# Storing result blocks from ScalarE's DMA queue instead of SyncE's, in a relational GNN layer with layer normalisation

## Chip, cores and metric

The kernel runs on one core of a Trainium2 chip. The metric is the device time of one execution in microseconds. The engines are called PE (TensorE), DVE (VectorE), ACT (ScalarE), POOL (GpSimd) and SP (SyncE).

## What is computed

There are 50,000 nodes with 256 features, 12,500 edges in eight relations, sorted by destination. Each node gets its own features, the product with a loop weight, and the sum of the messages of its incoming edges; the row is then normalised.

```
hx = jnp.einsum('ni,rio->rno', x, weight)
msg = hx[edge_type, src]
agg = jax.ops.segment_sum(msg, dst, num_segments=num_nodes)
node_repr = agg * 0.5 ** 0.5 + h_bias + (x @ loop_weight) * 0.5 ** 0.5
out = layernorm(x + node_repr)
```

## The kernel before

Work goes in pairs of tiles of 128 rows. There are three kinds. A main pair (m, 196 of them) takes 256 consecutive rows of x through the loop weight (with the identity added for the residual), the bias and the normalisation. A message pair (g, 53) gathers the sources of 256 edges of one relation each tile, multiplies by the relation's weight and scatters the messages into a table in DRAM. A fix pair (f, 50) redoes the rows that receive messages: it gathers x rows, multiplies, adds the sum of the messages by a matmul with a matrix of equal keys, normalises, and scatters the rows over the output that the main pairs stored before.

The order of the pairs is written out by hand as phases, and every engine walks the same list (`walk` with its own `step`): 66 m; then "gmgmgmm" repeated and "gmm" five times; six m; then f and m in turn ("fm"), and at the end four m and four f. While the first 66 main pairs run, POOL sorts the edges by relation with 98 indirect DMAs (line 647). The m pairs run from rows in blocks of four tiles: block b is the pairs 2b and 2b+1, loaded into `x_in` and finished in `y_out`, both rings of `BLOCK_RING` = 4 blocks. There are 97 full blocks of 512 rows and a last one of 336.

What each engine does for a pair: SP loads blocks of x (line 494), messages (532) and keys (524). POOL gathers (624), scatters messages (715) and fixed rows (664). PE transposes (1170), two pairs ahead of its own multiplication (1193), and adds the messages (1215). ACT copies the transposes out of PSUM (1053), moves messages (1084), carries one row from a fix tile to the next (1068), takes the deviation (1095) and normalises in place (1104), which counts up `normed`. DVE makes the low part of the split (892), adds the bias while moving the product out of PSUM (971 for m, 976 for f), and makes statistics (986, 939) and the factors (918, 928).

SP stores the blocks. In its step for the odd pair of block b it waits until PE has turned that pair, issues the load of block b+4, then waits until block b-2 (`LATE` = 2) is normalised, and issues its store (line 570). After the walk it stores the last two; the last block goes in two parts (567, 568). In a fix step SP waits for the pair's product before it loads the messages of the fix pair four further on, so its steps follow PE's. A store counts up `stored` of its slot. DVE waits for it before it adds into the slot again, four blocks later; POOL waits for it before it scatters fixed rows over rows that the main pairs wrote, and SP at the end. The fix pairs before the last three wait only for blocks long before theirs; the last three wait for all blocks.

Each engine's instructions run in the order in which its step issues them. PE, DVE and ACT hold four products in PSUM (`Y_RING`) between them.

Of the kernel before, what the change touches and what calls it, by code (L numbers as in the profile page):

```python
# [33 lines left out]
P = 128  # L34
# [6 lines left out]
BLOCK_RING = 4  # L41
LATE = 2
# [127 lines left out]
def gnn_layernorm_kernel(nc, x, src, dst, rel, weight, bias, loop_weight, out):  # L170
    N, D = x.shape
# [15 lines left out]
    BROWS = 4 * P  # L187
    BLOCKS = N // BROWS
# [69 lines left out]
    with ExitStack() as ctx:  # L258
# [164 lines left out]
        def block_rows(table, b):  # L423

            return table[bass.ds(b * BROWS, BROWS), :].rearrange("(p t) d -> p t d", t=4)
# [54 lines left out]
        def _(sp):  # L480
# [53 lines left out]
            def step(p):  # L534
                if p.kind == "f":
                    slot = p.fixed("f") % 4
                    following = p.count("f") + 4
                    if p.looped or following < FPAIRS:
                        sp.wait_ge(product, p.count("mgf") + 1)
                        load_messages(following * 2, slot)  # L540
                    if slot == 3:
                        unit = p.turns("f", 4)
                        uslot = (p.fixed("f") // 4) % 2
                        if p.looped or unit + 2 < UNITS:
                            sp.wait_ge(same_built, (unit + 1) * UNIT)
                            load_keys(unit + 2, uslot)
                after_p = p.ahead(5)
                if not p.looped and after_p is not None and after_p.kind == "f" and after_p.count("f") == 0:

                    for i in range(2):  # L550
                        sp.wait_ge(scattered[i], 32 * ((MPAIRS + 1 - i) // 2))
                    for f in range(min(4, FPAIRS)):
                        load_messages(2 * f, f)
                if p.kind != "m" or p.fixed("m") % 2 == 0:
                    return
                b, slot = p.turns("m", 2), (p.fixed("m") // 2) % BLOCK_RING
                if p.looped or b + 4 <= BLOCKS:
                    sp.wait_ge(turned, p.count("mgf") + 1)
                    load_block(b + 4, slot)
                if p.looped or b >= LATE:  # L560
                    store_block(b - LATE, (slot - LATE) % BLOCK_RING, nth(p, "m", -2 * LATE))

            def store_block(b, slot, ends):

                sp.wait_ge(normed, ends.count("mf") + 1)
                if isinstance(b, int) and b == BLOCKS:
                    sp.dma_start(out[b * BROWS:b * BROWS + 2 * P, :].rearrange("(p t) d -> p t d", t=2), y_out[:, slot, 0:2, :]).then_inc(stored[slot], 16)
                    sp.dma_start(out[N - REST:N, :], y_out[0:REST, slot, 2, :]).then_inc(rest_stored, 16)
                else:
                    sp.dma_start(block_rows(out, b), y_out[:, slot, :, :]).then_inc(stored[slot], 16)  # L570

            walk(sp, phases, step)
            end = Pair(phases, len(phases) - 1, 0, phases[-1].size - 1)
            for b in range(BLOCKS + 1 - LATE, BLOCKS + 1):
                store_block(b, b % BLOCK_RING, nth(end, "m", 2 * (b - BLOCKS) - 1))
            sp.wait_ge(rest_stored, 16)
            for i in range(BLOCK_RING):
                sp.wait_ge(stored[i], 16 * ((BLOCKS + BLOCK_RING - i) // BLOCK_RING))
# [464 lines left out]
        @block.scalar  # L1043
        def _(act):
            def copy_xt(p):

                if p is None:
                    return
                n, slot = p.count("mgf"), p.fixed("mgf") % Y_RING
                act.wait_ge(turned, n + 1)  # L1050
                wait(act, product, n - Y_RING + 1)
                to = xt_full if p.plain else xt_high
                nc.scalar.activation(to[:, slot, :], xt_ps[slot % XT_RING][:, :], ACT.Copy).then_inc(copied, 1)  # L1053

            def carry(p, t):

                if p is None or p.kind != "f":
                    return
                if not has_carry(p, t):
                    return  # L1060
                nxt = p if t == 0 else nth(p, "f", 1)
                slot = nxt.fixed("f") % 4
                act.wait_ge(message_loaded[slot], 32 * (nxt.turns("f", 4) + 1))
                if t == 0:
                    act.wait_ge(tile_sum, p.count("f") + 1)
                else:
                    act.wait_ge(product, p.count("mgf") + 1)
                nc.scalar.activation(message_in[0:1, 2 * slot + 1 - t, :], product_tile(p, t)[0:1, :], ACT.Copy).then_inc(carried, 1)  # L1068

            def fill_keys(p):  # L1070

                if p is None or p.kind != "f" or p.fixed("f") % 4:
                    return
                slot = (p.fixed("f") // 4) % 2
                act.wait_ge(keys_loaded[slot], 16 * (p.turns("f", 8) + 1))
                nc.scalar.activation(keys[:, slot, :, 0], keys[:, slot, :, RUN], ACT.Copy).then_inc(keys_filled, 1)

            def move_message(p):
                if p is None or p.kind != "g":
                    return  # L1080
                q, slot = p.fixed("mgf") % Y_RING, p.fixed("g") % 2
                act.wait_ge(product, p.count("mgf") + 1)
                wait(act, scattered[slot], 32 * p.turns("g", 2))
                nc.scalar.activation(message_out[:, 2 * slot:2 * slot + 2, :], y_ps[q][:, :].rearrange("p (t d) -> p t d", t=2),  # L1084
                                     ACT.Copy, scale=C).then_inc(message_moved, 1)

            def deviation(p):

                if p is None or p.kind == "g":
                    return  # L1090
                g, slot, half = ln_group(p)
                if half == 0:
                    return
                act.wait_ge(moments, (g + 1) * 4)
                nc.scalar.activation(std[:, slot, :], mean_var[:, slot, :, 1], ACT.Sqrt, bias=eps[:, 0:1]).then_inc(std_ready, 1)

            def norm(p, t):
                if p.kind == "g":
                    return
                g, slot, half = ln_group(p)  # L1100
                if t == 0:
                    act.wait_ge(scale_ready, g + 1)
                i = 2 * half + t
                a = nc.scalar.activation(y_tile(p, t), y_tile(p, t), ACT.Identity, scale=rstd[:, slot, i:i + 1], bias=shift[:, slot, i:i + 1])  # L1104
                if t == 1:
                    a.then_inc(normed, 1)

            act.wait_ge(pool_consts, 12)
            first_pair = Pair(phases, 0, 0, 0)
            for d in range(6):  # L1110
                copy_xt(first_pair.ahead(d))
            for d in range(2):
                deviation(first_pair.ahead(d))

            def step(p):
                carry(p.ahead(4), 0)
                copy_xt(p.ahead(6))
                part = split_part(p, 0)
                if part is not None:
                    act.wait_ge(weights_in, 32)  # L1120
                    nc.scalar.activation(w_rel_high[:, part:part + PART], w_rel[:, part:part + PART], ACT.Copy).then_inc(rel_high, 1)
                deviation(p.ahead(2))
                norm(p, 0)
                carry(p.ahead(4), 1)
                move_message(p.ahead(4))
                norm(p, 1)
                fill_keys(p.ahead(10))

            walk(act, phases, step)

            with act.If(needs_repair(act)):
                act.wait_ge(repair_open, 1)
                with act.Fori(0, FTP) as i:
                    act.wait_ge(repair_turned, i + 1)
                    past(act, act_past)
                    nc.scalar.activation(xt_full[:, 0, 0:D], xt_ps[0][:, 0:D], ACT.Copy).then_inc(repair_copied, 1)
                    act.wait_ge(repair_var, i + 1)
                    past(act, act_past)
                    nc.scalar.activation(std[:, 0, 0:1], mean_var[:, 0, 0, 1:2], ACT.Sqrt, bias=eps[:, 0:1]).then_inc(repair_std, 1)
                    act.wait_ge(repair_scale, 2 * i + 2)  # L1140
                    past(act, act_past)
                    nc.scalar.activation(repair_y, repair_y, ACT.Identity, scale=rstd[:, 0, 0:1], bias=shift[:, 0, 0:1]).then_inc(repair_result, 1)
# [147 lines left out]
```

## Time and profile before

| | us |
|---|---|
| median of 3 runs | 781.48 |
| lowest, highest | 780.89, 785.09 |
| span of the profiled execution | 1004.9 |
| busy in it: PE, PE's weight loads | 728.6, 662.7 |
| busy in it: DVE, POOL, ACT | 587.2, 537.1, 506.7 |
| DMA traffic | 173.78 MB |

The profiled execution is the only one with a trace; its span is all that is known of its own time, and it is much longer than the runs. Its durations of single operations can be used, its idle times only with care. In the trace a time is given from the start of the span; an instruction that issues a DMA is not counted as busy, and its duration is that of the issue, not of the transfer.

### The profile page before, as it was taken

How to read it: one execution, taken by the hardware profiler on the slowest of the kernel's cores; microseconds unless marked ns; L12 is line 12 of the kernel's file. 1: busy time of each engine (PE TensorE's matmuls, PEld its weight loads, DVE VectorE, ACT ScalarE, POOL GpSimd, SP SyncE). 2: the span in 40 equal slices, each digit the busy share in tenths (PEclk: the TensorE clock that was granted, in tenths of full speed). 3: DMA queues.
4: the chain of work that ended last, by engine and by line, in shares of the span. 5: the costliest groups of instructions: out<-in, count | busy, mean ns of one | idle time of the engine just before them, and what ended most of it. 6: DMA issues, size and time to landing. Idle time of an engine off the chain costs nothing. (4 is left out here: it accounts for less than half of the span.)

```text
span 1004.9 us, 18114 instructions
## 1 busy us (share of the span) xinstructions
PE 728.6 (73%) x4680; PEld 662.7 (66%) x4680; DVE 587.2 (58%) x1911; ACT 506.7 (50%) x1089; POOL 537.1 (53%) x610
## 2 busy tenths in 40 slices
PE   4643324899987778786877889887778777568880
PEld 4522213799977677786866779886668766567770
DVE  6621003899964355564555568876666655565771
ACT  2310102788865455454544457764646554555662
POOL 1677776100166656765666566365555556555633
PEclk9855556899998988987989899997898888898996
DMA  5511102777765555655564565765466556466531
GB/s 201 194 43 43 43 1 93 243 253 273 265 205 183 184 159 191 182 196 177 184 200 167 174 199 178 260 193 179 157 204 194 160 192 201 156 203 209 187 145 45
DMA packets 82706, 173.78 MB, mean 173 GB/s; under 512 B 28994, under 2 KB 45092, under 8 KB 82635
## 3 DMA queue, kind: packets, MB, share of 16 engines
q1 hardware_dynamic: 59675, 125.35, 37.1%
q0 software_dynamic: 22960, 47.58, 15.0%
q8 instruction: 33, 0.54, 0.2%
q14 instruction: 38, 0.31, 0.1%
HBM read 100.92 MB, written 78.67 MB: 179 GB/s over the span
## 5 line engine op out<-in xcount | busy, mean ns | idle before, releaser
L971 DVE TENSOR_TENSOR y_out<-y_ps,bias_b 128x512 f32<-128x512 f32 x196 | 134.3, 685 | 212.8 <-remote 153.9
L1193 PE MATMUL y_ps<-w_low,xt_high 128*128 128x256 f32 x768 | 253.0, 329 | 5.3 <-issue 5.1
L1104 ACT ACTIVATE y_out<-y_out,shift,rstd 128x256 f32<-128x256 f32 x392 | 216.7, 590 | 52.5 <-issue 37.1
L1193 PE MATMUL y_ps<-w_high,xt_high 128*128 128x256 f32 x768 | 230.8, 300 | 10.1 <-issue 10.1
L1193 PE MATMUL y_ps<-w_high,xt_low 128*128 128x256 f32 x768 | 231.1, 301 | 3.6 <-issue 3.2
L1170 PE MATMUL xt_ps<-ident,x_in 128*128 128x128 f32 x784 | 135.1, 301 | 121.5 <-DVE xt_low L892 54.2
L892 DVE TENSOR_TENSOR xt_low<-xt_ps,xt_high 128x512 fp32r<-128x512 f32 x221 | 150.2, 679 | 107.3 <-ACT xt_high L1053 73.2
L1053 ACT ACTIVATE xt_high<-xt_ps 128x512 fp32r<-128x512 f32 x221 | 129.1, 585 | 142.5 <-remote 108.8
L1170 PEld LDWEIGHTS xt_ps<-ident,x_in 128*128 128x128 f32 x784 | 102.7, 155 | 145.2 <-issue 89.7
L624 POOL DMA_INDIRECT gathered<-in_x,src_stage x106 | 109.2, 1030 | 130.5 <-PE xt_ps L1170 95.0
L1193 PEld LDWEIGHTS y_ps<-w_low,xt_high 128*128 128x128 f32 x768 | 161.3, 210 | 8.5 <-issue 7.8
L1193 PEld LDWEIGHTS y_ps<-w_high,xt_high 128*128 128x128 f32 x768 | 160.0, 208 | 9.7 <-issue 9.7
L1193 PEld LDWEIGHTS y_ps<-w_high,xt_low 128*128 128x128 f32 x768 | 161.5, 210 | 6.2 <-issue 5.5
L715 POOL DMA_INDIRECT message_rows<-message_out,edge_stage x106 | 108.6, 1024 | 88.9 <-ACT message_out L1084 60.5
L986 DVE BATCH_NORM_STATS2 stats<-y_out 128x6 f32<-128x256 f32 x392 | 147.6, 418 | 4.1 <-issue 0.4
L1193 PE MATMUL y_ps<-w_main,xt_full 128*128 128x256 f32 x432 | 120.0, 406 | 11.6 <-issue 8.1
L624 POOL DMA_INDIRECT gathered<-in_x,fix_src_stage x80 | 82.6, 1033 | 77.5 <-PE xt_ps L1170 46.0
L1215 PE MATMUL y_ps<-message_in,same 128*128 128x256 f32 x200 | 67.5, 421 | 71.6 <-ACT message_in L1068 50.9
L647 POOL DMA_INDIRECT grouped<-entry_stage,place_stage x98 | 95.4, 974 | 37.6 <-issue 29.0
L1068 ACT ACTIVATE message_in<-y_ps 1x256 f32<-1x256 f32 x99 | 36.6, 370 | 135.3 <-remote 78.4
L1193 PEld LDWEIGHTS y_ps<-w_main,xt_full 128*128 128x128 f32 x432 | 84.2, 206 | 27.5 <-issue 17.5
L1215 PEld LDWEIGHTS y_ps<-message_in,same 128*128 128x128 f32 x200 | 36.2, 202 | 80.9 <-ACT message_in L1068 55.9
(122 smaller groups left out, 927.7 us busy)
## 6 DMA issues: line engine op xcount, KB each, us to landing
x_in<-in_x SPq DMA_DIRECT2D x97, 512.0 KB
out_rows<-y_out SPq DMA_DIRECT2D x97, 512.0 KB
message_in<-message_rows SPq DMA_DIRECT2D x100, 128.0 KB
keys<-padded_dst SPq DMA_DIRECT2D x13, 508.0 KB
w_rel<-in_L_gnn_weight SPq DMA_DIRECT2D x1, 2048.0 KB, 14.3
gathered<-in_x,src_stage POOLq DMA_INDIRECT x106
message_rows<-message_out,edge_stage POOLq DMA_INDIRECT x106
grouped<-entry_stage,place_stage POOLq DMA_INDIRECT x98
```

What stands on the lines that cost most here:

```text
L624: nc.gpsimd.indirect_dma_start(gathered[:, 2 * slot + t, :], None, x, bass.IndirectOffsetOnAxis(ap=at_list[:, column:column + 1], axis=0), ...
L647: nc.gpsimd.indirect_dma_start(grouped, bass.IndirectOffsetOnAxis(ap=place_stage[:, k:k + 1], axis=0), entry_stage[:, k, :], None, bounds_ ...
L715: nc.gpsimd.indirect_dma_start(message_rows, bass.IndirectOffsetOnAxis(ap=edge_stage[:, column + t:column + t + 1], axis=0), message_out[: ...
L892: nc.vector.tensor_tensor(xt_low[:, slot, :], xt_ps[slot % XT_RING][:, :], xt_high[:, slot, :].bitcast(F32), ALU.subtract).then_inc(low_do ...
L971: nc.vector.tensor_tensor(to, y_ps[q][:, :].rearrange("p (t d) -> p t d", t=2), bias_2, ALU.add).then_inc(moved, 1)
L986: nc.vector.bn_stats(stats[:, slot, 2 * half + t, :], y_tile(p, t)).then_inc(stats_done, 1)
L1053: nc.scalar.activation(to[:, slot, :], xt_ps[slot % XT_RING][:, :], ACT.Copy).then_inc(copied, 1)
L1068: nc.scalar.activation(message_in[0:1, 2 * slot + 1 - t, :], product_tile(p, t)[0:1, :], ACT.Copy).then_inc(carried, 1)
L1104: a = nc.scalar.activation(y_tile(p, t), y_tile(p, t), ACT.Identity, scale=rstd[:, slot, i:i + 1], bias=shift[:, slot, i:i + 1])
L1170: last = nc.tensor.transpose(xt_ps[q % XT_RING][:, t * D + k * P:t * D + (k + 1) * P], rows[t][:, k * P:(k + 1) * P], ident[:, :])
L1193: return nc.tensor.matmul(to, xt[:, q, t * D + k * P:t * D + (k + 1) * P], w, start=start, stop=stop)
L1215: last = nc.tensor.matmul(to, same[:, 2 * slot + t, :], message_in[:, 2 * slot + t, :], start=False, stop=True)
```

## The change

The stores move from SP's list of instructions to ACT's. ACT calls `store` at the end of its step. In the step of the even m pair of block b+1, after normalising it, it waits for `normed` of the previous m pair and stores block b. The last block is stored in the step of the first of the four closing fix pairs. SP keeps its loads and the waits at its end. The contents and sizes of the stores, the semaphores that they count up, and those who wait for these stay as they are.

```diff
@@ SP's step @@
                     load_block(b + 4, slot)
-                if p.looped or b >= LATE:
-                    store_block(b - LATE, (slot - LATE) % BLOCK_RING, nth(p, "m", -2 * LATE))
-
-            def store_block(b, slot, ends):
-
-                sp.wait_ge(normed, ends.count("mf") + 1)
...
             walk(sp, phases, step)
-            end = Pair(phases, len(phases) - 1, 0, phases[-1].size - 1)
-            for b in range(BLOCKS + 1 - LATE, BLOCKS + 1):
-                store_block(b, b % BLOCK_RING, nth(end, "m", 2 * (b - BLOCKS) - 1))
@@ ACT @@
+            def store_block(b, slot, ends):
+
+                act.wait_ge(normed, ends.count("mf") + 1)
+                if isinstance(b, int) and b == BLOCKS:
+                    act.dma_start(out[b * BROWS:b * BROWS + 2 * P, :].rearrange("(p t) d -> p t d", t=2), y_out[:, slot, 0:2, :]).then_inc(stored[slot], 16)
+                    act.dma_start(out[N - REST:N, :], y_out[0:REST, slot, 2, :]).then_inc(rest_stored, 16)
+                else:
+                    act.dma_start(block_rows(out, b), y_out[:, slot, :, :]).then_inc(stored[slot], 16)
+
+            def store(p):
+
+                if p.kind == "f" and p.at == len(phases) - 1 and p.ahead(-1).kind == "m" and p.ahead(-1).count("m") == MAIN - 1:
+                    store_block(BLOCKS, BLOCKS % BLOCK_RING, p.ahead(-1))
+                if p.kind != "m" or p.fixed("m") % 2 or not p.looped and p.count("m") < 2:
+                    return
+                slot = (p.fixed("m") // 2 - 1) % BLOCK_RING
+                store_block(p.turns("m", 2) - 1, slot, nth(p, "m", -1))
...
                 norm(p, 1)
                 fill_keys(p.ahead(10))
+                store(p)
```

## Rows read from the trace of the kernel before

**Rows 1.** Spans and clock of the cores; then the page's transfer rates, 40 equal slices.

```profile
core 0: 1004.9 us, clock 0.854
...
GB/s 201 194 43 43 43 1 93 243 253 273 265 205 183 184 159 191 182 196 177 184 200 167 174 199 178 260 193 179 157 204 194 160 192 201 156 203 209 187 145 45
```

**Rows 2.** The page's busy time of each engine, share of the span, instructions.

```profile
PE 728.6 (73%) x4680; PEld 662.7 (66%) x4680; DVE 587.2 (58%) x1911; ACT 506.7 (50%) x1089; POOL 537.1 (53%) x610
```

**Rows 3.** Stretches: length, busy PE, PEld, DVE, ACT, POOL, clock, DMA share, GB/s.

```profile
180.00:260.00 80.00, 79.31 (x555) 74.63 (x555) 77.18 (x265) 68.78 (x139) 0.43 (x3) 0.96 0.75 261
...
820.00:910.00 90.00, 63.35 (x401) 58.11 (x400) 53.83 (x191) 46.68 (x110) 49.58 (x54) 0.85 0.56 179
```

**Rows 4.** Timeline of POOL, fix stretch: start, length, what, idle before and releaser.

```profile
896.61 1.04 POOL L624 DMA_INDIRECT gathered<-in_x,fix_src_stage  x1 [0.30 <-issue]
...
901.90 1.04 POOL L624 DMA_INDIRECT gathered<-in_x,fix_src_stage  x1 [0.30 <-issue]
```

**Rows 5.** Timeline of ACT, fix stretch: two deviations, one round apart.

```profile
889.73 0.30 ACT L1095 ACTIVATE std<-mean_var,eps 128x4 f32<-128x4 f32 x1
...
894.56 0.30 ACT L1095 ACTIVATE std<-mean_var,eps 128x4 f32<-128x4 f32 x1
```

**Rows 6.** Waits of the engines and of SP: us in total, times, longest.

```profile
POOL gathered L624 <- PE xt_ps L1170: 143.8, 29, 89.0
POOL message_rows L715 <- ACT message_out L1084: 60.5, 19, 4.1
...
POOL fix_src_stage L679 <- DVE y_fix L976: 31.7, 8, 5.5
...
POOL gathered L624 <- remote: 21.2, 12, 2.3
...
DVE y_out L971 <- DMA out_rows<-y_out: 2.5, 1, 2.5
...
SPq L570 <- ACT y_out L1104: 231.0, 53, 42.7
```

**Rows 7.** Timeline of POOL: sorting starts, first gather after it, first message pair.

```profile
27.02 0.19 POOL L641 COPY place_stage<-work 128x7 int32<-128x7 int32 x1 [21.41 <-DVE work L847]
...
169.92 1.06 POOL L624 DMA_INDIRECT gathered<-in_x,src_stage  x1 [0.88 <-POOL src_stage L658]
...
269.38 1.02 POOL L624 DMA_INDIRECT gathered<-in_x,src_stage  x1 [88.95 <-PE xt_ps L1170]
```

**Rows 8.** Timelines of SP, ACT and DVE, main pairs only (from 185.31 to 256.83 SP issues 19 stores).

```profile
185.31 0.35 SPq L570 DMA_DIRECT2D out_rows<-y_out  x1
...
189.39 0.35 SPq L570 DMA_DIRECT2D out_rows<-y_out  x1
190.04 1.09 ACT L1104 ACTIVATE y_out<-y_out,shift,rstd 128x256 f32<-128x256 f32 x2
190.29 0.34 SPq L494 DMA_DIRECT2D x_in<-in_x  x1
...
195.02 0.68 DVE L971 TENSOR_TENSOR y_out<-y_ps,bias_b 128x512 f32<-128x512 f32 x1
...
256.83 0.35 SPq L570 DMA_DIRECT2D out_rows<-y_out  x1
```

**Rows 9.** Everything on `y_out`: duration ns least/median/most, first and last start; landing.

```profile
L971 DVE TENSOR_TENSOR y_out<-y_ps,bias_b x196: 671/684/694, 23.6 to 970.6; 128x512 f32<-128x512 f32 x196
L570 SPq DMA_DIRECT2D out_rows<-y_out x97: 4/350/892, 37.3 to 976.4; - x97
...
DMA to landing us min/median/max: 3.4/3.4/3.4
```

**Rows 10.** Timelines of the tail: the last block's second part, ACT, POOL.

```profile
981.34 0.43 SPq L568 DMA_DIRECT2D out_rows<-y_out  x1
...
981.71 1.09 ACT L1104 ACTIVATE y_fix<-y_fix,shift,rstd 128x256 f32<-128x256 f32 x2 [0.77 <-DVE shift L928]
...
983.68 0.97 POOL L664 DMA_INDIRECT out_rows<-y_fix,fix_at  x1 [11.80 <-DMA out_rows<-y_out]
...
986.23 0.97 POOL L664 DMA_INDIRECT out_rows<-y_fix,fix_at  x1 [0.31 <-issue]
```

More of the change, by code:

```diff
@@ L559, in step @@
                     load_block(b + 4, slot)
-                if p.looped or b >= LATE:
-                    store_block(b - LATE, (slot - LATE) % BLOCK_RING, nth(p, "m", -2 * LATE))
-            def store_block(b, slot, ends):
-                sp.wait_ge(normed, ends.count("mf") + 1)
[L566 to L570, printed above, removed]
             walk(sp, phases, step)
-            end = Pair(phases, len(phases) - 1, 0, phases[-1].size - 1)
-            for b in range(BLOCKS + 1 - LATE, BLOCKS + 1):
-                store_block(b, b % BLOCK_RING, nth(end, "m", 2 * (b - BLOCKS) - 1))
             sp.wait_ge(rest_stored, 16)
```

## Prediction, made before the changed kernel was run

> **What bounds the kernel now.** I read the spans first, then busy time, the stretches, the waits of each engine, and last the timelines. The profiled execution spans 1004.9 us against a median of 781.48 us for the runs, so it is 223 us longer than what is to be predicted [rows 1]. The page's transfer rates say where: from 50 to 150 us (four slices of 25 us) it moves 43 GB/s or less, against 243 to 273 a little later [rows 1]. Durations of single instructions I take from the trace; idle time in it I do not trust as idle time of an ordinary run.
>
> No engine is busy all the time; PE leads with 73% [rows 2]. In the opening stretch where only main pairs run, PE is busy 79.31 of 80 us, and a block of two pairs takes (256.83 - 185.31)/18 = 3.97 us, 1.99 us a pair [rows 3, 8]. Later PE falls to 63 of 90 us [rows 3]. What is steady there is POOL. A fix pair costs it two gathers and two scatters, and a round with nothing to wait for takes 901.90 - 896.61 = 5.29 us [rows 4]. A message pair issues four such DMAs too. Meanwhile the other engines need 894.56 - 889.73 = 4.83 us for the main and the fix pair that belong to such a round [rows 5], and 7/3 pairs x 1.99 = 4.6 us a message pair.
>
> To see whether POOL sets the end, I take out of the span what POOL waited for in it: 143.8 (PE), 60.5 (ACT), 31.7 (DVE) and 21.2 us (unnamed) [rows 6]. 1004.9 - 257.2 = 747.7 us is POOL's own work with start and tail. That is 96% of 781.48; at most 33.8 us of waiting of this kind fit into an ordinary run, and some of it has to be there: the six main pairs between messages and fixes, and the first fix pairs. So POOL bounds the kernel nearly from end to end: sorting first (27.02 to 169.92 us), then messages, then fixes [rows 7]. The 88.95 us that POOL waits at 269.38 [rows 7] are the opening stretch, stretched by profiling: at 1.99 us a pair PE turns the first message pair 64 pairs after the first addition (23.6 us [rows 9]), at 151 us, 19 us before POOL's first gather.
>
> **The change, part by part.** *Removed from SP:* 97 stores of 512 KB and the two of the last block, a median of 350 ns each, and the waits ahead of them, 231.0 us [rows 6, 9]. Behind those waits stand loads of x four blocks ahead and of messages four fix pairs ahead. The waiting lists of PE, ACT and DVE name no such load in the steady part; their cover is those rings, 8 pairs or 16 us. Gain: 0. Without that cover a load would gain what SP waits there, 231.0/53 = 4.4 us at a time.
>
> *Added on ACT:* 99 DMA issues, each behind a wait on `normed` for the previous main pair. That pair was normalised one step earlier in ACT's own order, so the wait is met when ACT comes to it; behind it stand the next step's copy of the transposes (PE waits for it), the deviation and the normalising. ACT issues no DMA in this trace, so the cost is bounded by SP's rows: below by 0, if the issue passes under the two activations still running, and above by 0.89 us, the longest on SP [rows 9]. I take 0.35. All 99 on the path would be 35 us, and at 0.89 each 88 us. But they lie beside POOL: a store comes once in two fix rounds, where ACT's side has 2 x (5.29 - 4.83) = 0.92 us to spare, and in the message stretch more. It counts only where POOL waits for the others: the six main pairs and first four fix pairs (5 stores) and the last main pairs (2). 7 x 0.35 = 2.5 us at most; part of each lies under activations, so I take 1.0. Address arithmetic for the loop index is in that too.
>
> The Trainium skill ("Perfetto Trace Analysis", Per-instruction lifecycle) says the sequencer's part of such a DMA contains a wait for a generator locked by one sequencer at a time; no row here shows it, as only SP issues. By it an issue could double to 0.70 us.
>
> *Moved in time:* a store of block b is issued after the even pair of block b+1. In the opening stretch SP issues one at 189.39, and ACT is in the next normalising from 190.04 to 191.13, so the new issue falls between these: 0.6 to 1.7 us later [rows 8]. In the fix stretch SP reaches the store of b only after pair 2b+5 and the fix pair's product; ACT reaches it at 2b+2, so there it comes earlier. Who waits: DVE's addition that takes the slot again, four blocks on, and POOL's scatters. For DVE: the one landing on show took 3.4 us, for 80 KB behind 256 KB [rows 9]; 512 KB at 261 GB/s [rows 3] makes it some 4.1. A store of 189.39 has then landed at 193.5, and the addition to that slot is at 195.02 [rows 8], 1.5 us to spare. After the change 0.9 us are left, or 0.2 are missing. Cost 0, covered by the ring; cover gone is the first rival.
>
> *The tail:* the last block is now stored by ACT in the step of the first closing fix pair, whose normalising starts at 981.71; SP issued the second part at 981.34 [rows 10]. ACT's sequencer can be there at about 981.8 for the first part and 982.2 for the second, 0.8 us later, or 1.5 if it waits for both activations to end. Landing goes from 984.7 to 985.5, or 986.2. POOL needs this block only for the pair at 986.23; the two scatters from 983.68 wait for the normalising that ends at 982.80, not for the store [rows 10]. From a release to a POOL DMA lie about 0.9 us (982.80 to 983.68), so POOL can start at 986.4 to 987.1: 0.2 to 0.9 us late. I take 0.5.
>
> *Sum:* 0 + 1.0 + 0 + 0.5 = +1.5 us, at least 0, at most 2.5 + 0.9 = 3.4. From 781.48: **783.0 us**; the three runs themselves lie from 780.89 to 785.09. Half a percent, 3.9 us, is about what a measurement of this kernel can tell from no change.
>
> **Rivals.** *Slower: the slots of y_out in the opening stretch.* Loads and stores now sit in two queues. A load of 512 KB at the 261 GB/s of that stretch [rows 3] takes 2.0 us; SP issues one at 190.29 [rows 8], ahead of the new store. If the store has to share with it, it lands up to 2.0 us later, and the addition would have to wait 1.1 to 2.2 us. A block grows by about half of that, since store and addition lie some two blocks of this pace apart: 0.6 to 1.1 us. Over 33 blocks that is 20 to 36 us, of which POOL's sorting covers 19. The point from which it decides is 19/33 = 0.58 us a block; midway (0.85) it gives 781.5 + 28 - 19 = 790.5 us, at most 798.5. For it: the thin margin. Against it: today's margin with loads alongside left one DVE wait of 2.5 us in all [rows 6], and half of the load is through when the store starts. Chance 0.08.
>
> The Trainium skill ("DMA: Bandwidth & Descriptors", Queues, rings and completion order) says that a DMA engine takes turns between the queues that have work, packet by packet. No row here shows hardware queues side by side; by that rule the store would share and this rival would hold at its lower end, where the sorting hides it.
>
> *Slower: ACT becomes the bound of the fix stretch.* It needs more than 0.92 us a store. At 1.5 us, 25 stores cost 25 x 0.58 = 15 us: 796 us. For it: ACT feeds PE with copies and carries, so its delays pass on. Against it: 0.35 median, 0.89 longest. Chance 0.09.
>
> *Faster: SP was late after all.* If SP's waits delay message or x loads in an ordinary run, where engines run closer together, freeing SP returns some of the 33.8 us of POOL's waiting; one wait of 4.4 us at the start of the fixes and one in the tail give 781.5 + 1.5 - 8.8 = 774 us. Against it: no engine waits for such a load beyond the start. Chance 0.08.
>
> *It does something else than it says:* with the store at the pair's end ACT could stall on `normed`. The semaphore belongs to the previous pair, so I give no chance to it beyond the second rival.
>
> **How the numbers follow.** Forecast 0.75 at 783.0, own range 780 to 786. Rivals 0.08, 0.09, 0.08. The range reaches to about half of the rivals on either side: 778 to 789. Faster by over 0.5%: 0.07 (the third rival, nearly). Slower: the two slower rivals less their mild cases, 0.13, plus 0.04 from the forecast's upper end: 0.17. The rest, 0.76, within.
>
> **What would show it.** Right: POOL's rounds stay at 5.29 us; SP has no wait for normalising and ACT's issues take 0.3 to 0.5 us with the next activation hardly later; DVE has no more than a few us of waits for stores; the pair of scatters after the first two of the tail starts 2.7 to 3.4 us after them, in place of 2.55. Wrong: ACT rounds of the fix stretch above 5.29 us; DVE waiting for the store at each block of the opening; POOL's total of waits for ACT or DVE growing in fix rounds. The forecast fails as a whole if POOL was not the bound, that is, if the profile's waits that I took out belong to ordinary runs as well.

## The result and the profile after

The changed kernel takes 775.18 us (median of 4 runs, 774.27 to 775.80) against 781.40 us before (4 runs, 780.89 to 785.09). The ratio is 0.991, 95% interval 0.989 to 0.993: 6 us faster. Forecast were 783.0 us and a range of 778 to 789, with 7% for faster by over half a percent. The prediction was wrong.

The traced execution of the changed kernel spans 774.0 us and took 775.8 us, so unlike the one before its idle times can be believed. First its transfer rates and busy times (core, then the page's sections 1 and 2):

```profile
core 0: 774.0 us, clock 0.968
```

```profile
PE 656.6 (85%) x4680; PEld 611.4 (79%) x4680; DVE 578.3 (75%) x1911; ACT 500.4 (65%) x1089; POOL 535.3 (69%) x610
...
GB/s 206 224 270 214 225 218 218 218 224 192 249 214 230 200 228 214 221 214 214 235 202 210 240 233 182 290 271 244 259 270 238 256 248 209 281 253 259 210 165 34
```

The stretch of 43 GB/s [rows 1] is gone; it is missing in the second trace of the kernel before too, so it belonged to that one traced execution. The waits that answer [rows 6] (who waited for whom: us in total, times, longest):

```profile
POOL gathered L610 <- PE xt_ps L1174: 18.7, 15, 3.4
...
POOL message_rows L701 <- ACT message_out L1070: 2.8, 9, 0.3
...
POOL list_at L642 <- DMA grouped<-entry_stage,place_stage: 5.5, 1, 5.5
...
DVE y_out L957 <- DMA out_rows<-y_out: 20.8, 12, 3.1
...
SPq L494 <- PE xt_ps L1174: 397.9, 65, 18.6
```

POOL waits for PE 18.7 us and for ACT 2.8 us where [rows 6] has 143.8 and 60.5; a second trace of the kernel before, read below, has 31.8 and 0.6. So most of those were waits of that one traced execution. SP has no wait for normalising any more. But DVE now waits 20.8 us, in twelve places, for stores, and POOL 5.5 us for its own small writes at the end of the sorting. A comparison needs a trace of the kernel before that is as close to its time.

### The profile page after: what moved, and what is told of

The parts are those of the page before. It is cut to its first block and busy times, and to the rows that moved or that the text cites. A ratio compares the mean times of both kernels' runs of the same rounds, so it can differ in the third digit from the quotient of the medians.

```text
span 774.0 us, 18120 instructions
## 1 busy us (share of the span) xinstructions
PE 656.6 (85%) x4680; PEld 611.4 (79%) x4680; DVE 578.3 (75%) x1911; ACT 500.4 (65%) x1089; POOL 535.3 (69%) x610
## 5 line engine op out<-in xcount | busy, mean ns | idle before, releaser
L1197 PE MATMUL y_ps<-w_low,xt_high 128*128 128x256 f32 x768 | 238.7, 311 | 0.0
L1197 PE MATMUL y_ps<-w_high,xt_high 128*128 128x256 f32 x768 | 217.9, 284 | 0.0
L1197 PE MATMUL y_ps<-w_high,xt_low 128*128 128x256 f32 x768 | 217.8, 284 | 0.0
L957 DVE TENSOR_TENSOR y_out<-y_ps,bias_b 128x512 f32<-128x512 f32 x196 | 133.6, 682 | 34.1 <-DMA out_rows<-y_out 20.8
L1174 PE MATMUL xt_ps<-ident,x_in 128*128 128x128 f32 x784 | 122.2, 280 | 43.2 <-DVE xt_low L878 29.4
L1197 PEld LDWEIGHTS y_ps<-w_high,xt_low 128*128 128x128 f32 x768 | 148.3, 193 | 0.7
L1197 PEld LDWEIGHTS y_ps<-w_low,xt_high 128*128 128x128 f32 x768 | 148.1, 193 | 0.7
L1197 PEld LDWEIGHTS y_ps<-w_high,xt_high 128*128 128x128 f32 x768 | 147.1, 192 | 0.0
L1174 PE MATMUL xt_ps<-ident,gathered 128*128 128x128 f32 x412 | 64.7, 281 | 49.0 <-DVE xt_low L878 16.8
L1174 PEld LDWEIGHTS xt_ps<-ident,gathered 128*128 128x128 f32 x412 | 47.4, 143 | 56.2 <-issue 39.7
L650 POOL DMA_INDIRECT out_rows<-y_fix,fix_out_stage x72 | 72.8, 1011 | 21.9 <-issue 18.9
```

The lines of the kernel that those rows point to most:

```text
L650: nc.gpsimd.indirect_dma_start(out, bass.IndirectOffsetOnAxis(ap=at_list[:, column:column + 1], axis=0), y_fix[:, slot, t, :], None, bound ...
L957: nc.vector.tensor_tensor(to, y_ps[q][:, :].rearrange("p (t d) -> p t d", t=2), bias_2, ALU.add).then_inc(moved, 1)
L1174: last = nc.tensor.transpose(xt_ps[q % XT_RING][:, t * D + k * P:t * D + (k + 1) * P], rows[t][:, k * P:(k + 1) * P], ident[:, :])
L1197: return nc.tensor.matmul(to, xt[:, q, t * D + k * P:t * D + (k + 1) * P], w, start=start, stop=stop)
```

## The experiments

**Both kernels traced again.** The first pair of runs has no edit.

> The kernel before, unchanged, traced again, to have a trace of it whose span is near its time. If POOL set the end as in the trace of after, POOL's fix rounds are 5.29 us here too, and the 6 us that the change gave back stand in single places: POOL's waits at the start of the messages, at the start of the fixes, at the staging of the lists, or in the tail. If instead SP's blocked loads held the engines back all the time, POOL's rounds are longer than 5.29 us all through, or PE, ACT or DVE show waits for loads of x or messages. Time expected: 781 us.

> The changed kernel, unchanged, traced again on the same chip, for a trace beside that of the kernel before. Expected: 775 us, POOL's waits for PE, ACT and DVE after 180 us within a few us of the first trace of it.

Measured: 780.68 us with a span of 778.8 for the kernel before, 775.42 us with a span of 773.6 for the changed one. POOL issues the same 510 indirect DMAs in both, so their starts can be laid side by side. The start in the changed kernel is later (+) or earlier (-) than before by:

```
first gather after the sorting      +4.1 us
last gather before the fixes       +3.8 us, between 3.3 and 4.2 from the first on
gather of the second fix pair      +3.0 us
gather of the third fix pair       -6.3 us
gather of the fourth fix pair      -5.6 us, within 0.1 of it until the tail
last scatter of the kernel         -5.2 us
```

So nearly all of the difference is made in two places, against each other. The first is the opening. POOL waits for its sorting writes, then gathers (timelines of POOL, before and after):

```profile
165.89 0.60 POOL L656 DMA_DIRECT2D list_at<-grouped  x1 [1.76 <-DMA grouped<-entry_stage,place_stage]
...
169.33 1.06 POOL L624 DMA_INDIRECT gathered<-in_x,src_stage  x1 [0.88 <-POOL src_stage L658]
```

```profile
169.94 0.59 POOL L642 DMA_DIRECT2D list_at<-grouped  x1 [5.54 <-DMA grouped<-entry_stage,place_stage]
...
173.41 1.06 POOL L610 DMA_INDIRECT gathered<-in_x,src_stage  x1 [0.88 <-POOL src_stage L644]
```

The last sorting DMA is issued at 163.16 and 163.43 us; what differs is how long the small writes need to land, 1.76 us or 5.54. The stretches from 152 us on (length, busy PE, PEld, DVE, ACT, POOL, clock, DMA share, GB/s), before and after, show what they have to get past:

```profile
152.00:180.00 28.00, 6.41 (x38) 6.38 (x39) 2.70 (x8) 3.52 (x8) 18.27 (x23) 0.57 0.23 65
```

```profile
152.00:180.00 28.00, 14.68 (x101) 13.69 (x100) 15.65 (x54) 12.71 (x28) 14.96 (x19) 0.78 0.56 174
```

Before, the 66 opening pairs are through at 152 us and the DMA engines have a mean busy share of 0.23 only. After, they still run, because DVE had to wait for stores: 16.9 us in eleven places from 26 to 165 us, against none (waits of DVE in that stretch, changed kernel):

```profile
DVE y_out L957 <- DMA out_rows<-y_out: 16.9, 11, 2.6
```

The second place is the start of the fixes. SP's timeline before:

```profile
472.48 0.34 SPq L570 DMA_DIRECT2D out_rows<-y_out  x1
482.18 3.66 SPq L532 DMA_DIRECT2D message_in<-message_rows  x8
485.88 1.24 SPq L494 DMA_DIRECT2D x_in<-in_x  x1
487.16 0.43 SPq L570 DMA_DIRECT2D out_rows<-y_out  x1
487.64 0.46 SPq L494 DMA_DIRECT2D x_in<-in_x  x1
488.14 1.12 SPq L570 DMA_DIRECT2D out_rows<-y_out  x1
```

From 472.8 to 482.2 SP waits until all messages are scattered (two waits, 4.0 and 5.3 us), then issues eight loads of them, and the store of block 68 stands behind both. It goes out at 487.16, 14.7 us after the store ahead of it. DVE needs its slot for block 72 (DVE's timeline before, then POOL's):

```profile
493.57 0.69 DVE L971 TENSOR_TENSOR y_out<-y_ps,bias_b 128x512 f32<-128x512 f32 x1 [7.30 <-DMA out_rows<-y_out]
```

```profile
502.39 1.00 POOL L624 DMA_INDIRECT gathered<-in_x,fix_src_stage  x1 [12.27 <-PE xt_ps L1170]
```

and in the changed kernel ACT stores the same blocks while SP still waits, and POOL waits less (ACT's timeline, then POOL's):

```profile
477.69 0.60 ACT L1090 ACTIVATE y_out<-y_out,shift,rstd 128x256 f32<-128x256 f32 x1 [0.38 <-DVE shift L914]
477.69 0.34 ACTq L1101 DMA_DIRECT2D out_rows<-y_out  x1
478.19 0.59 ACT L1090 ACTIVATE y_out<-y_out,shift,rstd 128x256 f32<-128x256 f32 x1
...
484.00 0.34 ACTq L1101 DMA_DIRECT2D out_rows<-y_out  x1
```

```profile
496.06 1.00 POOL L610 DMA_INDIRECT gathered<-in_x,fix_src_stage  x1 [2.90 <-PE xt_ps L1174]
```

DVE's wait of 7.30 us is not all of the 9.4. PE stood still with it, from 486.94 to 494.41 us, and its granted clock was at the lower level (1.2 GHz) from 491.6 to 498.4 us. The two products behind that wait take PE 4.64 us up to its next transposes (494.41 to 499.05), against 2.67 us (490.06 to 492.73) in the changed kernel, where the clock stays at the upper level (2.4 GHz). That is 2.0 us more, and 7.3 + 2.0 is about the 9.4 (PE's timeline, before and after):

```profile
494.41 2.05 PE L1193 MATMUL y_ps<-w_main,xt_full 128*128 128x256 f32 x4 [7.47 <-DVE y_out L971]
```

```profile
490.06 1.10 PE L1197 MATMUL y_ps<-w_main,xt_full 128*128 128x256 f32 x4
```

The theory is then: +4 us in the opening, -9.4 us (12.27 less 2.90) at the start of the fixes by freeing the stores from SP's wait for the messages. Its rival is that SP's relief pays a little everywhere. The next four kernels tell them apart.

**ACT's stores in the opening only.** `on_act` is asked in both engines' steps:

```diff
+        def on_act(p, b):
+            if p.looped:
+                return p.at == 0 and True or p.at == 6 and False
+            return 0 <= b < 33
...
-                if p.looped or b >= LATE:
+                if (p.looped or b >= LATE) and not on_act(p, b - LATE):
                     store_block(b - LATE, (slot - LATE) % BLOCK_RING, nth(p, "m", -2 * LATE))
```

> Blocks 0 to 32 (the opening main pairs) are stored by ACT, as in the change; all others by SP, as before. Theory (the gain comes at the start of the fix stretch, where SP's wait for the scattered messages holds its stores up; the opening loses some): the opening is as slow as in after, with about 17 us of DVE waits for stores, the list is loaded 3 to 4 us later, the 9 us at the start of the fixes are not gained: 781.4 + 3.7 = 785 us. Rival (the gain is spread over all stretches, as SP's other loads come earlier): about 779 us.

Measured: 786.21 us, ratio to before 1.004 (1.0015 to 1.0066). DVE waits for stores 17.2 us in the opening, and POOL waits 3.9 us for the sorting writes. The first gather is 2.4 us later than before, a little less than expected; the wait at the start of the fixes stays (14.25 us for PE). The opening alone makes the kernel slower, but not all of the 4 us stand in the opening. In its trace POOL is 2.2 us behind the kernel before up to the tail, and 6.8 us behind after this line, where the kernel before waits 2.40 us:

```profile
764.43 0.97 POOL L671 DMA_INDIRECT out_rows<-y_fix,fix_at  x1 [7.04 <-DMA out_rows<-y_out]
```

The view names a store, but ACT ends the normalising of the fix pair at 763.55, 0.9 us before: it is that pair that POOL waits for. So the opening's own cost is 2 to 2.5 us in this trace. In the tail this kernel does what the kernel before does; why its wait grew is taken up at the last run and stays open.

**ACT's stores after the opening only.** The same with 33 <= b < 98 and the loop of the fixes in place of the opening's.

> Blocks 0 to 32 are stored by SP, as before; 33 to 97 by ACT, as in the change. Theory: opening as fast as before and the gain of 9.4 us at the start of the fixes: 772 us, faster than both kernels. Rival (spread gain, an opening that matters to neither): 777 us.

Measured: 772.37 us, ratio 0.987 (0.984 to 0.990). There is no wait of DVE for a store, 1.8 us for the sorting writes, and POOL's wait for the third fix pair is 2.92 us.

**ACT's stores around the start of the fixes only.** 66 <= b < 75, neither loop.

> Only blocks 66 to 74, those stored around the change from messages to fixes, are stored by ACT, all others by SP. Theory: these nine carry the whole gain: 772 us, and no wait of DVE for a store above 3 us at the start of the fixes. Rival (spread gain): 9 of 98 stores, about 781 us.

Measured: 772.88 us, ratio 0.987 (0.983 to 0.991). Nine stores of 98 bring what all 65 of the run before bring. The gain is in one place.

**No store on ACT; SP's order changed.** The block that waits for the messages is moved behind the load and the store of its step:

```diff
                 if p.looped or b >= LATE:
                     store_block(b - LATE, (slot - LATE) % BLOCK_RING, nth(p, "m", -2 * LATE))
+                after_p = p.ahead(5)
+                if not p.looped and after_p is not None and after_p.kind == "f" and after_p.count("f") == 0:
+                    for i in range(2):
+                        sp.wait_ge(scattered[i], 32 * ((MPAIRS + 1 - i) // 2))
+                    for f in range(min(4, FPAIRS)):
+                        load_messages(2 * f, f)
```

> The kernel before, with every store on SP; in SP's step, only the wait for all scattered messages and the first eight loads of messages are moved behind the load of x and the store of the same step. Theory (head of the line on SP: the store of block 68 stood behind that wait of some 9 us): the store is out before the wait, DVE's wait of 7 us for it is gone, and the kernel is as fast as with ACT's stores from there: 772 to 774 us. Rival (a queue of its own is what helps, not the order): 781 us.

Measured: 772.41 us, ratio 0.988 (0.985 to 0.990). SP's timeline:

```profile
471.13 0.43 SPq L494 DMA_DIRECT2D x_in<-in_x  x1
474.62 0.34 SPq L570 DMA_DIRECT2D out_rows<-y_out  x1
481.62 4.73 SPq L532 DMA_DIRECT2D message_in<-message_rows  x8
486.39 0.43 SPq L494 DMA_DIRECT2D x_in<-in_x  x1
```

The store is out at 474.62, DVE's wait is 1.4 us and POOL's 3.51 us. The second queue is not what helps: one store had to pass one wait. A load of x passes it here too, but in the experiment above only stores do, and the time is the same. This kernel is faster than the one before the change, with the smallest edit. Its four runs (770.43 to 773.32 us) also lie under those of the changed kernel (774.27 to 775.80), though the two intervals of the ratio still touch.

What remained was why the opening loses: because the stores are later by a pair, or because they have a queue of their own.

**ACT stores at once.** The store moves into the step of the block's own odd pair:

```diff
-                if p.kind == "f" and p.at == len(phases) - 1 and p.ahead(-1).kind == "m" and p.ahead(-1).count("m") == MAIN - 1:
-                    store_block(BLOCKS, BLOCKS % BLOCK_RING, p.ahead(-1))
-                if p.kind != "m" or p.fixed("m") % 2 or not p.looped and p.count("m") < 2:
+                if p.kind != "m" or p.fixed("m") % 2 == 0:
                     return
-                slot = (p.fixed("m") // 2 - 1) % BLOCK_RING
-                store_block(p.turns("m", 2) - 1, slot, nth(p, "m", -1))
+                store_block(p.turns("m", 2), (p.fixed("m") // 2) % BLOCK_RING, p)
```

> All stores on ACT, as in the change, but block b is stored in the step of its own odd pair, right after its last normalising: ACT waits there for that activation to end, some 0.6 us, and the store goes out one main pair earlier than in after. It tells lateness from the second queue in the opening. If the lateness makes DVE wait (17 us of waits for stores in after's opening), they are gone and the list is loaded as early as before: 772 us. If sharing the DMA engines between two hardware queues makes it, the waits stay near 17 us: 775 us. If ACT's wait on its own activation costs much, ACT's rounds of the opening exceed 4.0 us a block: over 776 us.

Measured: 772.85 us, ratio 0.987 (0.985 to 0.989). No waits for stores, 1.8 us for the sorting writes. ACT's wait for its own activation shows up as 16.9 us in all, 0.5 us at a time, ahead of the copies, and costs nothing. A queue of its own does no harm by itself.

**SP stores a pair later.**

```diff
-                    store_block(b - LATE, (slot - LATE) % BLOCK_RING, nth(p, "m", -2 * LATE))
+                    store_block(b - LATE, (slot - LATE) % BLOCK_RING, nth(p, "m", 1 - 2 * LATE))
```

> All stores on SP, as before, but each waits for the normalising of one more main pair, so it is issued about when the change issues it. Lateness theory: DVE waits for stores in the opening as in after (some 17 us), the list is loaded about 4 us later, and the fix stretch begins as late as before: 785 us or more. Queue theory: an opening without such waits, 781 us.

Measured: 782.64 us, ratio 1.000 (0.9985 to 1.0007). The lateness reading missed: DVE waits 0.6 us for stores in the opening, not 17, and the time is that of the kernel before. Lateness by itself does no harm there, as a second queue by itself did none in the run above, so each reading alone is refuted by one of the two runs. The start of the fixes is worse: DVE waits 10.0 us for the store of block 68, and POOL waits 15.59 us for PE instead of 12.27. That store goes out at 487.44, only 0.3 us later than before, so its lateness does not explain all of this.

What remains is both together. On SP the next load of x comes behind the store in the same list, however late the store is. With two lists they are released by different things, and in the changed kernel both are issued at the same time, some stores just behind the load (timeline, SP and ACT):

```profile
106.04 0.33 SPq L494 DMA_DIRECT2D x_in<-in_x  x1
106.39 0.34 ACTq L1101 DMA_DIRECT2D out_rows<-y_out  x1
```

The packets of 4 KB of those two queues, counted in half microseconds from the trace's list of packets (SP's queue, ACT's queue):

```
107.0  15   0      109.5   4  46
107.5  17   0      110.0   0  52
108.0  33   0      110.5   0  38
108.5  27   0      111.0   0  42
109.0  32  10      111.5   0  24
```

The store's first packets leave 2.9 us after its issue, when the load is nearly done, and its last ones 4.4 us after it; from 110.5 on the right column counts those of the next store too. DVE gets the slot at 112.05, 5.7 us after the issue and 1.64 us too late:

```profile
112.05 0.69 DVE L957 TENSOR_TENSOR y_out<-y_ps,bias_b 128x512 f32<-128x512 f32 x1 [1.64 <-DMA out_rows<-y_out]
```

**The changed kernel, with the loads held behind the stores.**

```diff
                     load_block(b + 4, slot)
+                if p.looped or b >= LATE:
+                    sp.wait_ge(normed, nth(p, "m", 1 - 2 * LATE).count("mf") + 1)
+                    past(sp, sp_past)
```

> The changed kernel, with SP made to wait, after each load of x, for the main pair whose normalising ACT's next store follows, so that the next load is issued at or after that store and never ahead of it; no store is moved. Theory (in the opening a late store loses to the load that is issued beside it): with the loads held back DVE's waits for stores in the opening fall from 17 us to a few us, the list is loaded as early as before the change, and the kernel gains some 3 us on after: 772 us. Rival (two queues on one set of DMA engines slow each other whatever the order): the waits stay, 775 us. It also holds SP's message loads back a little in the fix stretch, which may cost there.

Measured: 773.63 us, ratio 0.989 (0.986 to 0.991). ACT's stores and SP's loads now lie apart:

```profile
100.11 0.34 ACTq L1104 DMA_DIRECT2D out_rows<-y_out  x1
101.29 0.33 SPq L494 DMA_DIRECT2D x_in<-in_x  x1
```

DVE has no wait for a store, and the first gather is at 169.56 us, 3.85 us earlier than in the changed kernel. With the two runs before it, that shows the cause of the opening's loss: stores as late as in the change, in a queue of their own, cost nothing there if no load gets ahead of them. The time itself did not follow in full: against the changed kernel's 0.991 (0.989 to 0.993) the intervals overlap. POOL's timeline shows where the lead went:

```profile
751.77 0.97 POOL L653 DMA_INDIRECT out_rows<-y_fix,fix_at  x1 [4.89 <-DMA out_rows<-y_out]
```

The changed kernel has this line at 752.28 with 2.60 us of waiting. The lead had grown to 5.3 us by the start of the fixes. There 2.6 us of it went: POOL waits 5.69 us for PE, which itself waits 1.86 us for a load of x, against 0.54 us in the changed kernel, and has the lower clock from 495.1 to 498.5 us. Another 2.1 us went in the tail, where POOL waits for the first of the last fix pairs to be normalised (at 750.88; the view names a store). In this trace, and in those of the stores after the opening and around the fixes, PE's granted clock stood at its lower level for 3.4 us from 701 to 703 us on, shortly before the tail; in that of the reordered SP it did not, and there POOL's line stands at 747.04. That drop cannot be the only reason: with ACT storing at once the clock falls for the last time before the tail from 678.9 to 685.8 us, and POOL still waits 4.95 us there. One more kernel points to the clock, the one with ACT's stores in the opening only: its clock is low from 713.4 to 720.2 us, and its wait of 7.04 us is the longest of all. Over the traces this wait runs from 2.40 to 7.04 us; what sets it was not tried, and differences of 2 to 3 us between single traces can come from it.

## Why the prediction was wrong, point by point

*POOL bounds the kernel: right.* With a trace near the run's time, POOL's rounds in the fix stretch are 5.31 us (517.24 to 522.55 in the kernel before, 516.98 to 522.29 after), and between the two places above POOL's starts move by less than 1 us against those of the kernel before. In the tail it is held up by the others, for 2.40 us before and 2.60 us after in the second pair of traces.

*SP's relief is worth nothing: the step that failed.* The prediction took the waits of SP at the stores and asked what stands behind them. It had to ask the other way round too: what do the stores stand behind? The answer is SP's wait for the scattered messages, one of 4.4 us in the trace before, too small in its list to catch the eye, and then eight loads. The margin that was computed for a slot in the opening, 1.5 us, was never set against a wait in SP's list. Its price is 9.4 us, 7.3 of them DVE's wait for that store and 2.0 PE's lower clock after it. The third rival named the place ("at the start of the fixes"), and at 774 us came within about 1 us of the result. That closeness is luck: its 8.8 us were to come from two waits for loads, one of them in the tail, and the 4 us that the opening cost are not in it. It got 0.08, because no engine showed a wait for a load. The wait that mattered was DVE's for a store. In the trace of before it could not be seen: a single wait of 2.5 us, as the engines were held up everywhere.

*The moved store in the opening costs nothing: wrong by 4 us.* The first rival was true as a mechanism: 16.9 us over 33 blocks, 0.51 us a block, below the point of 0.58 from which it was to decide. It costs anyway, because the cover was taken as a block of 19 us that hides all or nothing. Main pairs that run on beside the end of the sorting slow its small writes, 5.54 us against 1.76; in each of the six other kernels without DVE's waits of 17 us in the opening they take 1.7 to 1.8 us, and in the one with 17.2 us of them 3.9. The rule of the Trainium skill that was weighed there ("DMA: Bandwidth & Descriptors", Queues, rings and completion order) has queues taking turns packet by packet. Where packets of both are under way, the trace fits that: from 112.5 to 113.0 us each queue sends 23. But in the example no store packet leaves for 2 us while the load runs, and the trace does not show what holds the store back. The first rival had the store share with the load from its start; here it comes mostly after the load instead.

*ACT's issue: right.* 0.34 us in the median, beside a running activation (477.69 above), and POOL's rounds stay as they were; the term of +1.0 us shows nowhere. The longest of the 97 stores is 0.41 us, so a doubling by a locked generator, as weighed from the Trainium skill ("Perfetto Trace Analysis", Per-instruction lifecycle), does not show in them.

*The tail, +0.5 us: small, as forecast, but hardly by that path.* Laid side by side, POOL's last eight scatters lose 0.3 us. The two scatters that wait for the last block start 2.62 us after the two ahead of them, against 2.55 before and 2.7 to 3.4 forecast, so the later store of that block is worth less than 0.1 us of it.

*Sum:* +1.5 us was forecast. Of the measured -5.2 us in the pair of traces, +4 and -9.4 are the two terms valued at 0. The own range of 780 to 786 rested on both.

## What to carry to other kernels

When an instruction leaves an engine's list, look not only at who stood behind it but at every wait that it stood behind, once for each seam between stages: here one wait of some 9 us at a seam outweighed a hundred issues of 0.34 us. Before a queue is added, try the order in the one there is; here moving one wait behind one store brought all of the gain and none of the loss in the opening. And a cover that ends in a shared resource leaks: work delayed into the end of a covered stretch can slow what covered it.

## What the runs showed of the hardware

Two transfers of 512 KB issued up to 0.36 us apart from SP's and ACT's queues went mostly one after the other in the order of issue, not side by side. From 60 to 140 us in the changed kernel, a store issued 0.16 to 0.36 us behind a load sent its first packet 2.7 to 3.4 us after its issue; one issued 0.14 to 0.15 us ahead of a load did so after 0.9 to 1.1 us. From 45 to 150 us, of the half microseconds with traffic of either queue only 20% (36 of 178) hold 8 or more 4 KB packets of each; where the store was issued 0.39 us or more ahead of the load (ACT stores at once) it was 4% (8 of 199). A separate queue gives a transfer its own place in a list, not its own share of the engines at once. A DMA issue on ACT takes 0.34 us of its list while an activation runs on (median of 97, longest 0.41). And where PE had stood still for 7.47 us, its granted clock fell to the lower level for 6.8 us, and its next products took 4.64 us instead of 2.67.
